# Attention sum, skip term and sum over experts moved from TensorE to VectorE and ScalarE, in a kernel whose steps run in a periodic order

## What is computed

```python
# attention over the 8 points of a query (b = image, n = query, p = point, h = head)
keys   = einsum('bnpc,dc->bnpd', sampled, W_k)
values = einsum('bnpc,dc->bnpd', sampled, W_v)
attn   = softmax(einsum('bnhd,bnphd->bnhp', q, k) / sqrt(dh), axis=-1)
out    = einsum('bnhp,bnphd->bnhd', attn, v)        # the sum over points
h      = concatenate([out, txt], axis=1)
# the recurrence runs over the images; y is its read-out plus the skip term
y      = einsum('tbd,ed->tbe', ht, C_w).real + d_vec * x     # x = layernorm(h)
h      = h + y
# experts, on x = layernorm(h)
hidden = silu(x @ w1[e]) * (x @ w2[e])
expert_out = einsum('bseh,eho->bseo', hidden, w3)
h      = h + einsum('bseo,bse->bso', expert_out, dispatch)   # the sum over experts
```

## Time and profile before

| | us |
|---|---|
| median of 3 runs (2580.26 to 2585.14) | 2583.46 |
| time of the profiled execution | 2582.08 |
| its span, first to last instruction | 2580.2 |
| TensorE busy (matmuls) | 2425.4 (94%) |
| VectorE busy | 1679.8 (65%) |
| GpSimd busy | 1644.2 (64%) |
| ScalarE busy | 963.9 (37%) |
| DMA, mean share of the 16 engines | 48% |

### The profile page before, as it was taken

One profiled execution on the slowest core, in us unless ns is written; L12 is line 12 of the kernel. 1 busy time (PEld: TensorE's weight loads), 2 busy tenths in 40 slices (PEclk: granted clock), 3 DMA queues, 4 the chain that ended last, 5 costly groups with the idle time before them and its releaser, 6 DMA issues.

```text
span 2580.2 us, 48912 instructions
## 1 busy us (share of the span) xinstructions
PE 2425.4 (94%) x17937; PEld 2212.2 (86%) x17937; DVE 1679.8 (65%) x4050; ACT 963.9 (37%) x2118; POOL 1644.2 (64%) x2168
## 2 busy tenths in 40 slices
PE   2567999999999999999999999999999999999999
PEld 1455889999898999989999998999999898998888
DVE  1235767676777667676766767676676767667764
ACT  1122434344343434334343434434343443433332
POOL 0387858577585848758484875848487685858600
PEclk9986999999999999999999999999999999999998
DMA  9392917346281825628182562818255381722100
GB/s 226 91 257 66 249 55 211 105 130 198 64 253 42 226 84 150 180 72 245 39 229 81 157 175 78 240 39 227 80 164 168 91 229 41 219 74 77 55 4 6
DMA packets 362926, 346.95 MB, mean 134 GB/s; under 512 B 49088, under 2 KB 313408, under 8 KB 362560
## 3 DMA queue, kind: packets, MB, share of 16 engines
q1 hardware_dynamic: 313536, 209.54, 30.2%
q0 software_dynamic: 49152, 134.28, 17.8%
HBM read 205.84 MB, written 137.89 MB: 133 GB/s over the span
## 4 chain that ended last, share of the span: by engine, by line
PE 70%; DVE 11%; issue 9%; POOL 5%; ACT 4%; SPq 0%; DMA 0%; DVEq 0%; ACTq 0%; POOLq 0%
PE bank_o L587 16%; PE bank_h L577 9%; PE bank_d L669 8%; PE bank_h L578 7%; PE bank_d L679 7%; PE bank_a L725 5%; POOL gath L523 4%; PE bank_z L599 3%; DVE hid L963 2%; PE bank_a L710 2%; PE bank_p L637 2%; PE bank_p L635 2%; DVE wsam L1049 2%; PE bank_p L630 2%; POOL rest L530 1%
## 5 line engine op out<-in xcount | busy, mean ns | idle before, releaser
L523 POOL DMA_INDIRECT gath<-table,idx x1024 | 1099.8, 1074 | 270.3 <-issue 237.7
L577 PE MATMUL bank_h<-xsplit,w 128*128 128x384 f32 x1536 | 596.5, 388 | 25.6 <-DVE hid L963 21.3
L778 ACT ACTIVATE silu<-bank_h 128x384 f32<-128x384 f32 x768 | 380.2, 496 | 607.4 <-PE bank_h L578 549.8
L587 PEld LDWEIGHTS bank_o<-w_sb,hid 128*128 128x128 f32 x4608 | 553.6, 192 | 14.8 <-issue 12.9
L587 PE MATMUL bank_o<-w_sb,hid 128*128 128x64 f32 x4608 | 551.0, 273 | 1.3 <-DVE scaled L970 0.9
L578 PE MATMUL bank_h<-xsplit,w 128*128 128x384 f32 x1536 | 519.3, 338 | 0.0
L963 DVE TENSOR_TENSOR hid<-silu,bank_h 128x384 f32<-128x384 f32 x768 | 418.1, 549 | 109.0 <-ACT silu L778 85.8
L530 POOL MEMSET rest<- 1x400 f32 x1024 | 432.6, 422 | 29.6
L1049 DVE TENSOR_TENSOR wsam<-gath,cw 128x1024 f32<-128x1024 f32 x256 | 313.0, 1222 | 186.5 <-PE bank_d L669 145.6
L543 POOL TENSOR_TENSOR lns<-lns,neghalf 128x3 f32<-128x3 f32 x96 | 87.1, 907 | 435.9 <-DVE lns L940 435.8
L970 DVE TENSOR_TENSOR scaled<-bank_o,disp 128x512 f32<-128x512 f32 x288 | 198.6, 690 | 218.8 <-PE bank_o L587 211.6
(11 more groups left out here) (148 smaller groups left out, 2683.7 us busy)
## 6 DMA issues: line engine op xcount, KB each, us to landing
table<-pixmaj SPq DMA_DIRECT2D x80, 1024.0 KB
xin<-x_dram SPq DMA_DIRECT2D x256, 256.0 KB
table<-pixmaj SPq DMA_DIRECT2D x32, 960.0 KB
table<-pixmaj SPq DMA_DIRECT2D x16, 1088.0 KB
gath<-table,idx POOLq DMA_INDIRECT x1024
out_dram<-ob SPq DMA_DIRECT2D x48, 96.0 KB
gath<-w_dram SPq DMA_DIRECT2D x4, 512.0 KB, 8.6
interp_sb<-interp_dram SPq DMA_DIRECT2D x1, 1024.0 KB, 6.4
```

Of the source, the lines that this page charges most:

```text
L523: pool.indirect_dma_start(out=gath[buf][:, p, :, :].rearrange("p a c -> p (a c)"), out_offset=None, in_=table[par], in_offset=bass.Indirec ...
L577: mm(bank[:, 0:GC], w12[:, e, which, 0, :], xsplit[gp][:], start=True, stop=False)
L587: last = mm(bank_o[:, C * i:C * (i + 1)], hid[:, e, 128 * k:128 * (k + 1)], w3_sb[:, e, :], start=True, stop=True)
L778: nc.scalar.activation(silu[e % 2][:], bank_h[r][:, 0:GC], ACT.Silu).then_inc(silu_done, 1)
```

## The change

**Sum over experts.** `W` no longer uses one bank and one VectorE product. It has two banks, `bank_o[0]` and `bank_o[1]`, and ScalarE scales: eight ACTIVATEs of 128x64, each with the dispatch weight of one expert as scale, read per partition. `Z` becomes a step of VectorE: a tree of three additions over the eight scaled outputs (256, 128 and 64 elements a partition), the last into `part`. `M1` goes. `M2` on VectorE adds the two halves, then `h2`. `bank_z`, `zT`, four transposes per Z and six matmul instructions per M2 go.
**Skip term.** P3 gets a VectorE part that multiplies the normalised x by `d_row` (d_vec in all partitions) and adds it to `h_sb` in place. P4 loses the products with `d_diag`.
**Attention sum.** S3 becomes a step of VectorE, a tree of additions over the 8 points in place in `v_sb` (1024, 512 and 256 elements), and then the product with the denominator that S4 had. The transposes, the copy to `avT` and S4 go. D2 on TensorE no longer waits for `attn_done`.
**Order.** The positions in `schedule()` follow, and the shifts of W, M2, S3 and S4 go.

```diff
-    "W": {"dve": -0.19},
-    "M2": {"pe": 0.5, "dve": 0.5, "sp": 0.5},
-    "S3": {"act": 0.54},
-    "S4": {"pe": 0.25, "dve": 0.25},
...
-                put("W", 2, (g, half, k), pe=n, dve=n + 1.2)
-                put("Z", 2, (g, half, k), pe=n + 2.2)
+                put("W", 2, (g, half, k), pe=n, act=n + 0.6)
+                put("Z", 2, (g, half, k), dve=n + 1.6)
         n = NE * g + 23.7
-        put("M1", 2, (g,), act=n)
-        put("M2", 2, (g,), pe=n + 0.8, dve=n + 1.6, sp=n + 2.2)
+        put("M2", 2, (g,), dve=n, sp=n + 0.6)
...
-        put("P3", behind, (nxt,), pe=p + 5, act=p + 5.5)
+        put("P3", behind, (nxt,), dve=p + 3, pe=p + 5, act=p + 5.5)
...
-        put("S3", 1, (u,), pe=t + 3.5, act=t + 3.9)
-        put("S4", 1, (u,), pe=t + 4.4, dve=t + 5.1)
+        put("S3", 1, (u,), dve=t + 3.6)
...
-                        wait(pe, eo_scaled, n)
+                        wait(pe, eo_scaled, n - 1)
                         for i in range(8):
                             e = 8 * half + i
-                            last = mm(bank_o[:, C * i:C * (i + 1)], hid[:, e, 128 * k:128 * (k + 1)],
+                            last = mm(bank_o[n % 2][:, C * i:C * (i + 1)], hid[:, e, 128 * k:128 * (k + 1)],
                                       w3_sb[:, e, :], start=True, stop=True)
...
-                            mm(bank_p[:, C * k:C * (k + 1)], state[:, GC * g + 128 * k:GC * g + 128 * (k + 1)],
-                               c_st[:], start=True, stop=False)
-                            last = mm(bank_p[:, C * k:C * (k + 1)], xnT[:, 128 * k:128 * (k + 1)], d_diag[:],
-                                      start=False, stop=True)
+                            last = mm(bank_p[:, C * k:C * (k + 1)], state[:, GC * g + 128 * k:GC * g + 128 * (k + 1)],
+                                      c_st[:], start=True, stop=True)
...
-                            if j in (0, 5):
-                                wait(pe, attn_done, 2 * b + (j == 5))
...
-                            wait(act, av_turned, 2 * b - 2 + j // 4 + 1)
+                            wait(act, attn_done, 2 * b - 2 + j // 4 + 1)
...
+                    elif kind == "W":
+                        g, half, k = args
+                        n = 2 * GT * (NGRP * b + g) + GT * half + k
+                        act.wait_ge(eo_ready, n + 1)
+                        act.wait_ge(disp_done, NGRP * b + g + 1)
+                        wait(act, pair_sum, n - 1)
+                        for i in range(8):
+                            e = 8 * half + i
+                            last = nc.scalar.activation(scaled[n % 2][:, i, :], bank_o[n % 2][:, C * i:C * (i + 1)],
+                                                        ACT.Identity, scale=disp[gpar(par, g)][:, k, e:e + 1])
+                        last.then_inc(eo_scaled, 1)
...
+                    elif kind == "Z":
                         g, half, k = args
+                        n = 2 * GT * (NGRP * b + g) + GT * half + k
+                        sums.start(n)
+                        dve.wait_ge(eo_scaled, n + 1)
+                        eo = scaled[n % 2]
+                        for m in (4, 2):
+                            link(sums, tt(eo[:, 0:m, :], eo[:, 0:m, :], eo[:, m:2 * m, :], ALU.add))
+                        tt(part[:, half, k, :], eo[:, 0, :], eo[:, 1, :], ALU.add).then_inc(pair_sum, 1)
+                    elif kind == "M2":
+                        g = args[0]
                         gp = gpar(par, g)
...
+                        link(mix, tt(ob[gp][:], part[:, 0, :, :], part[:, 1, :, :], ALU.add))
+                        tt(ob[gp][:], ob[gp][:], h2[g][:], ALU.add).then_inc(ob_done, 1)
...
+                    elif kind == "P3":
+                        g = args[0]
+                        skip.start(b, 2 * g)
+                        dve.wait_ge(xn_ready, 2 * NGRP * b + 2 * g + 1)
+                        own = h_sb[par][:, GT * g:GT * (g + 1), :]
+                        link(skip, tt(lnsq[:], lnx[:], spread(d_row[:], 1, GT), ALU.mult))
+                        skip.inc(tt(own, own, lnsq[:], ALU.add))
...
+                    elif kind == "S3":
+                        u = args[0]
+                        soft.start(b, SOFT_N * u + 4)
+                        dve.wait_ge(soft_v, soft.value())
+                        vw = v_sb[:, 4 * HEADS * u:4 * HEADS * (u + 1), :].rearrange("p (t n) c -> p t n c", t=4)
+                        for n in (4, 2, 1):
+                            link(soft, tt(vw[:, :, 0:n, :], vw[:, :, 0:n, :], vw[:, :, n:2 * n, :], ALU.add))
```

98 lines of the change are left out of this document (19 added, 79 removed).

## The result

The changed kernel takes 2685.16 us (median of 4 runs, 2678.71 to 2695.73) against 2583.49 us before: a ratio of 1.040 (95% interval 1.036 to 1.044), 102 us slower where 120 us faster was forecast. Its profiled execution took 2691.57 us. The page of the kernel after: span, TensorE's busy time, its granted clock in 40 slices (tenths of full speed), and the engines' shares of the chain that ended last.

A forecast was written before the change was run, and what follows sets the result against it. TensorE's in-order list was taken as the bound; with VectorE's list the longer in some stretches, steps fall 7.1 us to 142.5. 14 full steps give 99 us, the last two about 12 and 9: 120 us, so 2463 us, range 2345 to 2640.

The forecast's parts named there:

- TensorE's list: TensorE's work in a full step: 18.2 us removed, from 147.6 to 129.4 us.
- VectorE, ScalarE, GpSimd: Other engines' lists per full step: VectorE rises to 116.4 us, ScalarE to 91; GpSimd's instructions stay, with little room.
- rival 2: GpSimd's gather loop becomes the bound: a step of 147 us, 2526 us in all; chance 0.13.
- Holes: TensorE's waits in full steps: busy about 91%, holes ahead of X, most late in the step behind S3.
- the longer list in each stretch of four slots: How a full step was summed from TensorE's and VectorE's orders: mean 141.4 us, 142.5 with 1.1 added.
- The clock: TensorE's granted clock, 0.99 in the full stretch before; below 0.95 in full steps was named a sign of being wrong.
- Rival 4: TensorE's clock falls, low for 20% of the time: a step of about 152 us, 2600 us in all; chance 0.09.
- The last two steps: s = 16 and s = 17: gains of about 12 us and about 9 us.
- "Its clearest cost is delay": ScalarE's eight scalings: VectorE gets 1.9 us later what it got at the end of W.
- Rival 3: VectorE's waits don't shrink, falling only to 40 us: a step of 156.4 us, 2657 us in all; chance 0.16.
- The stretch named in the forecast: Slots 44 to 47, late in a full step: 12 us of VectorE work against 5.5 us on TensorE.

The follow-up runs named there:

- e2_skip: The kernel before with only the skip term moved to VectorE: 2542.4 us, ratio 0.984.
- e12_half_u0: The kernel before with the skip term and the u=0 half of the attention sum moved to VectorE, u=1 left on TensorE: 2516.7 us, ratio 0.974.
- e13_half_u1: The kernel before with the skip term and the u=1 half of the attention sum moved to VectorE, u=0 left on TensorE: 2621.8 us, ratio 1.015.
- e7_one_act: The changed kernel with one 128x512 copy on ScalarE in place of W's eight scalings, dispatch weights left out: 2622.7 us, ratio 1.015.
- e14_no_attn_order: The changed kernel with the attention sum left on TensorE, scalings behind the next silu and Z behind the next hid: 2606.1 us, ratio 1.009.
- e9_spread: The changed kernel with S2 earlier and S3's tree cut in two pieces, spread in VectorE's order: 2738.4 us, ratio 1.058.
- e5_tail_dense: The changed kernel with two extra unread 384-column matmuls ahead of every X of the last two images: 2671.1 us, ratio 1.033.

## Why the prediction was wrong, point by point

- **TensorE's list: right.** At the full clock 129.4 us a step was forecast. 139.9 were measured with some 24 us at the low level, which is 130.4 without it. The cleaner test is where the clock stayed up: e2_skip 143.0 against 147.6 - 4.3 = 143.3, e12_half_u0 141.0 against 140.7.
- **VectorE, ScalarE, GpSimd: near.** VectorE 114.8 us a step (forecast 116.4), ScalarE 85.8 (91), the eight scalings 1.57 us from start to next start (1.9), the mean gather 1094 ns (1100 to 1150). VectorE's wait for gathered rows ahead of D1 is 35.1 us in all, against 36.1 before, so the gather loop did not become the bound: rival 2 falls.
- **Holes: near in size by luck, and read as harmless.** 13.7 us against 13.1, most of them ahead of X for `hid`, with the longest behind S3, as forecast. But the forecast's holes were meant at the full clock, where the steps above point to some 20; the low clock fills a part of them. The taking of the longer list in each stretch of four slots was thus too kind: it was fitted to the kernel before, whose holes are 1.8 us a step. The failed step is that the putting together gave these holes no price beyond their own length.
- **The clock: the term that was left out of the sum.** The forecast step is 129.4 + 13.1 = 142.5, the measured one 130.4 + 9.5 + 13.7 = 153.6. Of the 11.1 us between them 9.5 are TensorE's time at the low clock. By the line through the full steps the clock is worth 6.3 of the 11.1 and longer holes the other 4.8. Over the full steps it is 14 x 11.1 = 155 us of the miss. Rival 4 had this mechanism (20% of the time low, 142 us for TensorE, 152 a step), and its size was near (16%, 139.9, 153.6), in part because its sum is 3 us short: 142 and the forecast's holes of 13.1 are 155 a step, which gives about 2640 and not 2600. Its chance of 0.09 was too low. The row that told it, has 22% idle and 0.70; I took it that a full stretch with a tenth of holes would be spared because X stands in every slot. X stands in every slot here too, and waits.
- **The last two steps: a failed step.** By work alone s = 16 was put at 121, and s = 17 at 9 us less than before. The prediction read s = 17 of the kernel before as about 110 us; from its last S2(u=1) to the end of the span it is 118.6, so the forecast is 109.6. They took 152.0 and 153.6, 75 us of the miss. With the full steps that makes 230 us, against 229.6 between 2462 and the profiled execution's 2691.6. There the longer list of each stretch does not set the time; the path from W through the scalings, silu or Z, and `hid` to X does, and its waits bring the clock down to 0.85 and 0.70. "Its clearest cost is delay" stood in the prediction, and no sum was made of it. Rival 4 leaves these steps out in the same way: with them its 2600 would have been 2675, and its 2640 2715.
- **Rival 3** had a step of 156.4 us from waits of 40 us on VectorE; they are 38.8. Its numbers are near, its mechanism is not: Z's wait is shorter than the one it replaced (123.8 against 218.8), and what grew is X's for `hid` (from 21.3 in the kernel before to 144.0).
- **The slots.** The stretch named in the forecast, with VectorE at twice TensorE's work, holds the longest waits, and e12_half_u0 against e13_half_u1 shows that the place decides what the attention sum's half costs.

What stays open: which wait brings the clock down in a given step, and what the experts' sum loses by in the full steps. Kernels with equal idle time differ in clock (e7_one_act 10.3 us and 0.90, e14_no_attn_order 9.8 and 0.96). And since no run sets the waits and the clock of full steps apart, the 9.5 and the 6.3 us are worked out from rows, not an experiment; e9_spread (same waits, lower clock, 3.9 us longer) and e5_tail_dense are the nearest to one.

## What to carry to other kernels

Work moved off the engine that is full can cost more than it brings where the receiving engine's list is the longer one in that very stretch: lay both lists out by stretches, and place or split the moved work by them (half of this attention sum gained 26 us, the other half cost 79). A TensorE that gets holes must be priced with its low clock on top, and first where the profile already shows it below 1. In stages with little work, at the end above all, sum the path from matmul to matmul through the other engines, and keep new operations behind those that the next matmul waits for.

## What the hardware showed beyond that

- The granted clock fell at 532.5 behind 22.50 us of which TensorE was busy for 19.99, with no wait over 1.2 us among them, and it stayed low for 24 us in which the engine was busy for 20.28. In the step of 1464.22 the same two short waits left it at the full level. Equal full steps of one execution differ by 5.6 us in length (150.3 to 155.9) with it.
- ScalarE's scalings of 128x64 out of PSUM with a scale per partition take 333 ns each, but eight of them pass in 1.57 us, 0.20 apart. The overlap is larger than the one read from copies in the earlier trace rows.
- VectorE's trees of two SBUF operands, 24 us a step of them, lengthened the mean gather by 20 ns only, 64 x 0.020 = 1.3 us a step. The Trainium skill (SBUF — State Buffer, "SBUF: two separate sides") has such operations hold up a GpSimd operation that reads SBUF. The trace agrees in kind, and puts the price of these short ones no higher than that.
